# Causal attention on one core: key-by-query weights of a fifth row tile go through DRAM, and an early product moves into the next head

## The chip, the cores and the metric

One core of a Trainium2 chip runs the whole program as one launch. The metric is the device time in microseconds, median of the runs. The engines are TensorE (PE, with PEld for its weight loads), VectorE (DVE), ScalarE (ACT), GpSimd (POOL), and SyncE (SP), which here issues every DMA. Each engine works through its own instructions strictly in the order of its program, and waits for semaphores of the others.

## The reference

One transformer block with adaptive layer norm, in fp32:

```python
h = _layernorm(x) * (1 + ca) + sa
q, k = rope(h @ wq), rope(h @ wk); v = h @ wv     # 32 heads, 8 key/value heads, T = 1024, HD = 128
scores = einsum('bhtd,bhsd->bhts', q, k) / sqrt(HD), masked to s <= t
att = softmax(scores); out = einsum('bhts,bhsd->bhtd', att, v)
x = x + ga * (out @ wo)
h = _layernorm(x) * (1 + cb) + sb
x = x + gb * (h @ W.T + b + low-rank term of the rank that a router picks)
```

## The kernel before, in words

Every fp32 matrix product is made of three products in a rounded format (fp32r): hi x hi, hi x lo, lo x hi. So each operand is split by a copy on ScalarE (the `_hi` part) and a subtraction on VectorE (the `_lo` part).

The program runs over 8 groups (one key/value head each) of 4 query heads. A head h has a `front` and a `back` on every engine, one function each in the block of the engine; all of them name the same steps in orders that are written out by hand. The queries of a head are 8 row tiles i of 128, tile i with its i+1 key blocks:

- `scores(h, i)` on TensorE, `masked(h, i)` on VectorE (adds the mask, finds the row maximum), `exp(h, i)` on ScalarE, `inverse(h, i)` on VectorE, `normalise(h, i)` on GpSimd.
- The weights must then lie with the keys on the partitions. For tiles 0 to 3 VectorE transposes blocks of 32x32 (`turn`) into the buffer `turned`; SyncE writes it to DRAM (`p_rows`) and reads it back in column order into `pa_lo` (`turn_columns`: one write, a wait for its landing, four reads); ScalarE and VectorE split it (`early_hi`, `early_lo`). For tiles 4 to 7 TensorE transposes each block into the PSUM banks `transposed` (`transposes`), and ScalarE and VectorE split each bank into `pb_hi` and `pb_lo` (`transposed_hi`, `transposed_lo`).
- `weighted(h, 0)`, called pva, multiplies the values with `pa`: the early product, at the end of the head's `back`. `weighted(h, 1)`, called pvb, does it with `pb`: the late product, in the `front` of the next head, after its tile 3's scores. `output_hi`, `output_lo` split both results.
- Between them lie filling jobs (`fill`): projections of q, k, v for the next head or group, output projections (`wo`) in the first head of a group. Weights of the projections come through two slots of `stage`, in the order of the lists `W_GROUP` and `W_LATE`; `split_hi` and `split_lo` split them, and the split of the load two places before frees a slot.

SyncE's program is one queue too: its loads and the turning of the columns stand in one written order, and a wait for a landing holds up every issue behind it.

## Time and profile before

| | |
|---|---|
| median of 3 runs | 1114.86 us (1112.5 to 1119.03) |
| the profiled execution's own time | 1113.62 us |
| its span, first to last instruction | 1111.8 us, mean granted clock 0.993 |
| busy share of the span | PE 95%, DVE 70%, ACT 57%, POOL 47% |
| DMA | 88.22 MB in 99004 packets, 79 GB/s |

A row of time gives the start and the length of an operation in us, then engine, line, operation, output and inputs, shapes and count, and in brackets the engine's idle time before it with the instruction that ended it. Matrix products overlap a little in such rows, so what a step takes is read from start to start.

### The profile page before, as it was taken

To read this page: it belongs to the slowest core of one execution; us is meant where nothing else is said; L and a number is where in the kernel's file an instruction comes from. 1 tells how busy PE (TensorE), PEld (TensorE's weight loads), DVE (VectorE), ACT (ScalarE), POOL (GpSimd) and SP (SyncE) were. 2 spreads that over 40 slices of the span, in tenths; PEclk is the share of its full clock that TensorE was granted. 3 is DMA by queue.
4 is the path that set the end of the run, shared out by engine and by line. 5 is a ranking of instruction groups with operands and counts; after the bars stand their busy time and mean duration, and the time that the engine had idled before them with its cause. 6 is when DMAs were issued, how large, how long until landed. Compare 5 with 4: busy or idle time off the path is not lost.

```text
span 1111.8 us, 16527 instructions
## 1 busy us (share of the span) xinstructions
PE 1055.0 (95%) x5416; PEld 867.1 (78%) x5416; DVE 775.7 (70%) x1834; ACT 635.4 (57%) x1298; POOL 521.9 (47%) x506
## 2 busy tenths in 40 slices
PE   6999999998999989999999999999999999998897
PEld 3668878887878878887878878887878878887775
DVE  4668866588558866588557865678647865678576
ACT  5547754477337654477437754477436753477433
POOL 2535553365425654365425643365425652455244
PEclk8999999999999999999999999999999999999999
DMA  6562323133302233033202233033212223024001
GB/s 212 152 216 67 103 79 76 39 95 95 78 18 68 85 96 76 34 98 97 71 25 67 86 95 77 12 109 99 57 49 67 77 86 95 3 97 130 10 20 57
DMA packets 99004, 88.22 MB, mean 79 GB/s; under 512 B 39460, under 2 KB 84644, under 8 KB 98792
## 3 DMA queue, kind: packets, MB, share of 16 engines
q1 hardware_dynamic: 98920, 87.17, 26.6%
q8 instruction: 44, 0.72, 0.3%
q14 instruction: 40, 0.33, 0.1%
HBM read 59.88 MB, written 27.26 MB: 78 GB/s over the span
## 4 chain that ended last, share of the span: by engine, by line
PE 56%; DVE 14%; ACT 12%; POOL 7%; issue 6%; DMA 4%; SPq 1%; POOLq 0%; DVEq 0%; ACTq 0%
PE accumulators L649 14%; PE accumulators L664 13%; PE accumulators L679 13%; PE scores L609 6%; PE transposed L622 6%; DVE p_large L1172 3%; POOL qc L1539 3%; ACT pb_hi L907 2%; ACT pa_hi L913 2%; DVE turned L1196 2%; POOL qr L1535 2%; DVE pb_lo L1184 2%; ACT qr L932 2%; PE scores L864 2%; ACT qr L931 2%
## 5 line engine op out<-in xcount | busy, mean ns | idle before, releaser
L907 ACT ACTIVATE pb_hi<-transposed 128x512 fp32r<-128x512 f32 (+3 forms) x256 | 117.5, 511 | 211.7 <-PE transposed L622 211.5
L1526 POOL TENSOR_SCALAR p_large<-p_large,rowinv 128x640 f32<-128x640 f32 (+3 forms) x128 | 125.1, 978 | 229.0 <-DVE rowinv L1177 229.0
L1535 POOL TENSOR_TENSOR qr<-qr,trig 128x512 f32<-128x512 f32 x80 | 104.4, 1305 | 221.1 <-ACT qr L932 221.0
L1184 DVE TENSOR_TENSOR pb_lo<-transposed,pb_hi 128x512 fp32r<-128x512 f32 (+3 forms) x256 | 138.9, 584 | 94.0 <-ACT pb_hi L907 93.6
L899 ACT ACTIVATE p_large<-p_large,negmax 128x640 f32<-128x640 f32 (+3 forms) x128 | 126.3, 986 | 87.6 <-DVE negmax L1172 87.5
L609 PE MATMUL scores<-k_hi,q_hi 128*128 128x512 f32 (+2 forms) x384 | 139.3, 363 | 1.7 <-DVE negmax L1172 1.7
L1172 DVE CUSTOM_DVE_ANT_0 p_large<-scores,mask 128x640 f32<-128x640 f32 (+3 forms) x128 | 129.4, 1011 | 4.0 <-PE scores L609 3.7
L609 PE MATMUL scores<-k_hi,q_lo 128*128 128x512 f32 (+2 forms) x384 | 131.4, 342 | 0.0
L609 PE MATMUL scores<-k_lo,q_hi 128*128 128x512 f32 (+2 forms) x384 | 131.1, 341 | 0.0
L1526 POOL TENSOR_SCALAR p_small<-p_small,rowinv 128x128 f32<-128x128 f32 (+3 forms) x128 | 97.2, 775 | 71.6 <-DVE rowinv L1177 71.6
L622 PE MATMUL transposed<-ident,p_large 128*128 128x128 f32 x832 | 113.9, 275 | 12.3 <-DVE pb_lo L1184 6.1
L622 PEld LDWEIGHTS transposed<-ident,p_large 128*128 128x128 f32 x832 | 93.8, 140 | 38.2 <-POOL p_large L1526 16.2
L1539 POOL TENSOR_TENSOR qc<-qc,qr 128x512 f32<-128x512 f32 x80 | 119.9, 1499 | 6.5 <-POOL qr L1535 0.3
L1249 DVE TENSOR_TENSOR y<-accumulators,y 128x512 f32<-128x512 f32 x64 | 43.5, 688 | 84.4 <-PE accumulators L679 84.4
L1223 DVE TENSOR_TENSOR qc<-accumulators,trig 128x512 f32<-128x512 f32 x80 | 55.2, 690 | 45.5 <-ACT qr L932 45.4
L609 PEld LDWEIGHTS scores<-k_hi,q_hi 128*128 128x128 f32 x384 | 72.5, 189 | 7.9 <-DVE negmax L1172 2.2
L609 PEld LDWEIGHTS scores<-k_hi,q_lo 128*128 128x128 f32 x384 | 72.3, 188 | 6.7
L679 PE MATMUL accumulators<-wo_hi,o_hi 128*128 128x512 f32 x256 | 71.1, 399 | 6.3 <-DVE y L1249 3.9
L609 PEld LDWEIGHTS scores<-k_lo,q_hi 128*128 128x128 f32 x384 | 72.9, 190 | 5.0
L899 ACT ACTIVATE p_small<-p_small,negmax 128x128 f32<-128x128 f32 (+3 forms) x128 | 71.0, 562 | 7.8 <-DVE negmax L1172 6.8
L664 PE MATMUL accumulators<-h_hi,wq_hi 128*128 128x512 f32 x256 | 69.3, 392 | 1.3 <-DVE ga_b L1282 1.3
L679 PE MATMUL accumulators<-wo_lo,o_hi 128*128 128x512 f32 x256 | 68.6, 390 | 0.0
(165 smaller groups left out, 2225.9 us busy)
## 6 DMA issues: line engine op xcount, KB each, us to landing
p_rows<-turned SPq DMA_DIRECT2D x32, 640.0 KB, 2.9
pa_lo<-p_rows SPq DMA_DIRECT2D x128, 160.0 KB, 3.1
stage<-in_L_attn_wq_dram SPq DMA_DIRECT2D x32, 256.0 KB, 2.8
stage<-in_L_attn_wo_dram SPq DMA_DIRECT2D x32, 256.0 KB, 2.7
v_rows<-vt SPq DMA_DIRECT2D x32, 128.0 KB, 2.2
v_lo<-v_rows SPq DMA_DIRECT2D x32, 128.0 KB, 3.1
y<-in_L_wmod_dram SPq DMA_DIRECT2D x4, 512.0 KB, 5.7
stage<-in_L_attn_wk_dram SPq DMA_DIRECT2D x8, 256.0 KB, 2.7
```

Source lines behind the costliest of these rows:

```text
L609: mm = nc.tensor.matmul(S_flat[:, c0 + key:c0 + key + n], a[:, i * P:(i + 1) * P], b[:, key:key + n], start=(k == 0), stop=(k == 2))
L622: mm = nc.tensor.transpose(TB[:, b, (j % 4) * P:(j % 4 + 1) * P], row(i)[:, j * P:(j + 1) * P], ident[:])
L649: mm = nc.tensor.matmul(acc[:, c0:HALF], v[:, j, :], pt, start=(hi and v is v_hi and j == 0), stop=(not hi and j == 4 * half + 3))
L664: mm = nc.tensor.matmul(acc, a[:, k, :], b[:, k, half * HALF:(half + 1) * HALF], start=(n == 0), stop=(n == 3 * KC - 1))
L679: mm = nc.tensor.matmul(acc, a[:, r, t * P:(t + 1) * P], b[:, r, :], start=(n == 0), stop=(n == 3 * R - 1))
L899: nc.scalar.activation(row(i), row(i), ACT.Exp, bias=negmax[:, i:i + 1], scale=-1.0, accum_out=rowsum[:, i:i + 1]).then_inc(s_exp, 1)
L907: nc.scalar.activation(pt_of(i, part, True), src, ACT.Copy).then_inc(t_hi, 1)
L1172: nc.vector.tensor_tensor_reduce(row(i), S_flat[:, c0:c0 + n], mask[:, T - n:T], -SCALE, 3.4e38, ALU.add, ALU.min, negmax[:, i:i + 1]).the ...
L1184: nc.vector.tensor_tensor(pt_of(i, part, False), src, f32(pt_of(i, part, True)), ALU.subtract).then_inc(t_lo, 1)
L1526: nc.gpsimd.tensor_scalar(row(i), row(i), rowinv[:, i:i + 1], 1.0, ALU.mult, ALU.mult).then_inc(s_norm, 1)
L1535: nc.gpsimd.tensor_tensor(qr[:, s, :], qr[:, s, :], trig[:, 1, half * HALF:(half + 1) * HALF], ALU.mult).then_inc(r_sin, 1)
L1539: nc.gpsimd.tensor_tensor(qc[:, s, :], qc[:, s, :], qr[:, s, :], ALU.add).then_inc(r_sum, 1)
```

## The change

Tile 4's weights no longer pass through TensorE. After `normalise(h, 4)` VectorE transposes them in blocks into the first half of `turned` (`turn_fourth`; it waits until the write of `p_rows` for this head has landed, since that reads the same buffer), SyncE writes them to `fourth_rows` and reads them back into `pb_lo`, and `fourth_hi` and `fourth_lo` split them in the next head's front, ahead of `transposed_hi` and `transposed_lo` of tile 7. The late product waits for `fourth_lo`. `pb` is laid out by tile, in runs of 32 columns like `pa`. The early product moves from the end of `back` to the next head's front, before tile 7's transposes. Some steps change places: `masked(h, 4)` stands before `output_lo` for h > 0, `early_lo` stands behind the output projections' additions for h = 0, the k weights are loaded and split before the fourth `wo` block. The end of the last group is ordered anew in the same sense (not shown).

```diff
         def pt_of(i, part, hi):
 
             js = parts(i)[part]
-            n = len(js)
...
-            return buf[:, at:at + 3 * (n - 1) + 1:3, :]
+            at = 7 * (i - 4) + js[0]
+            return (pb_hi if hi else pb_lo)[:, :, at:at + len(js), :].rearrange("p a l r -> p l a r")
         def pt_row(j, half, hi):
 
...
                 at = 1 + ROW_START[j]
                 return j * P, buf[:, :, at:at + 4 - j, :].rearrange("p a i r -> p i a r")
             buf = pb_hi if hi else pb_lo
...
+            if j == 7:
+                return 2 * P, buf[:, :, 13:29:15, :].rearrange("p a i r -> p i a r")
+            i0 = max(4, j)
+            at = 7 * (i0 - 4) + j
+            return (i0 - 4) * P, buf[:, :, at:at + 7 * (7 - i0) + 1:7, :].rearrange("p a i r -> p i a r")
...
         W_FIRST = [("k", 0), ("q", 0), ("v", 0)]
         W_GROUP = [("q", 1), ("q", 2), ("wo", 0), ("q", 3), ("wo", 1), ("wo", 2)]
-        W_LATE = [("q", 0), ("wo", 3), ("k", 0), ("v", 0)]
+        W_LATE = [("q", 0), ("k", 0), ("wo", 3), ("v", 0)]
...
+            def turn_fourth(n):
+
+                sp.wait_ge(fourth_turned, n + 1)
+                if n:
+                    sp.wait_ge(fourth_in, 64 * n)
+                sp.dma_start(fourth_rows, turned[:, 0:5 * P]).then_inc(fourth_out, 16)
+                sp.wait_ge(fourth_out, 16 * (n + 1))
+                if n:
+                    sp.wait_ge(a_full, N.of[("a", ("pvb", (n - 1) % R), (n - 1) // R)])
+                src = fourth_rows.rearrange("(a c) (b m) -> b c a m", a=4, b=4)
+                for b in range(4):
+                    sp.dma_start(f32(fourth_blocks(pb_lo)[32 * b:32 * b + 32]), src[b]).then_inc(fourth_in, 16)
...
@@ -548,6 +561,7 @@
             turn_columns(0)
             sp.wait_ge(a_full, N.value("a", ("mod", "sb"), g0))
             sp.dma_start(mod_w[:, :, 0:D], wmod_v[:, :, 2 * D:3 * D]).then_inc(mod_in[1], 16)
+            turn_fourth(0)
             sp.wait_ge(a_full, N.value("a", ("mod", "cb"), g0))
             sp.dma_start(mod_w[:, :, D:2 * D], wmod_v[:, :, 5 * D:6 * D]).then_inc(mod_in[2], 16)
             load(("q", 2), g0)
@@ -563,21 +577,25 @@
                     turn_value_rows(at)
                     load(("wo", 0), at)
                     turn_columns(R * g)
+                    turn_fourth(R * g)
                 load(("q", 3), at)
                 turn_columns(R * g + 1)
+                turn_fourth(R * g + 1)
                 load(("wo", 1), at)
                 load(("wo", 2), at)
                 turn_columns(R * g + 2)
+                turn_fourth(R * g + 2)
                 if g + 1 < GROUPS:
                     load(("q", 0), at, 1)
+                    load(("k", 0), at, 1)
                     load(("wo", 3), at)
-                    load(("k", 0), at, 1)
...
                 turn_columns(R * g + 3)
+                turn_fourth(R * g + 3)
...
                     steps = [(pa_hi_done, n, hi_lo[:2], range(4)), (pa_lo_done, n, hi_lo[2:], range(4))]
                 else:
                     first, second = (N.value("t", (h, 7, part), at, ahead) for part in range(2))
+                    pe.wait_ge(fourth_lo_done, head_number(h, at, ahead) + 1)
                     steps = [(t_hi, first, hi_lo[:2], range(4)), (t_lo, first, hi_lo[2:], range(4)),
                              (t_lo, second, hi_lo, range(4, 8))]
...
@@ -720,6 +739,7 @@
                 fill(h, 1, at)
                 scores(h, 2, at)
                 if h or not at.first:
+                    weighted(hb, 0, at, ahead)
                     transposes(hb, 7, at, ahead)
                 scores(h, 3, at)
                 if h or not at.first:
...
                 scores(h, 5, at)
                 fill(h, 3, at)
                 fill(h, 4, at)
-                transposes(h, 4, at)
                 scores(h, 6, at)
                 transposes(h, 5, at)
                 scores(h, 7, at)
                 fill(h, 5, at)
                 transposes(h, 6, at)
-                weighted(h, 0, at)
```

On ScalarE and VectorE (an increment's end and a second copy of the same lines are left out):

```diff
             def front(h, at):
                 hb, ahead = before(h, at)
-                if h or not at.first:
-                    output_hi(hb, 0, at, ahead)
                 fill(h, 1, at)
-                if h or not at.first:
-                    transposed_hi(hb, 7, at, ahead)
                 exp(h, 0, at)
                 exp(h, 1, at)
+                if h or not at.first:
+                    fourth_hi(hb, at, ahead)
+                    transposed_hi(hb, 7, at, ahead)
+                    output_hi(hb, 0, at, ahead)
                 exp(h, 2, at)
...
+                    split_hi(("k", 0), at, 1)
                     split_hi(("wo", 3), at)
-                    split_hi(("k", 0), at, 1)
...
+                elif i == 6:
+                    row_free = (fourth_turned, head_number(h, at) + 1)
                 else:
-                    row_free = (t_full, N.value("t", (h, i - 2, 1), at))
+                    row_free = (t_full, N.value("t", (h, 5, 1), at))
...
@@ -1191,9 +1215,24 @@
                     if i in tiles:
                         need(dve, s_norm, N.value("s", (h, i), at))
                         if n and i == 0:
-                            dve.wait_ge(rows_out, 16 * n)
+                            dve.wait_ge(fourth_out, 16 * n)
                         src = row(i)[:, js[0] * P:(js[-1] + 1) * P].rearrange("p (j b c) -> p j b c", b=4, c=32)
                         nc.vector.transpose(turned_blocks(i, js), src).then_inc(p_turned, 1)
+
+            def turn_fourth(h, at):
+
+                n = head_number(h, at)
+                dve.wait_ge(s_norm, N.value("s", (h, 4), at))
+                dve.wait_ge(rows_out, 16 * (n + 1))
+                src = row(4).rearrange("p (j b c) -> p j b c", b=4, c=32)
+                dst = turned[:, 0:5 * P].rearrange("p (b l r) -> p l b r", b=4, r=32)
+                nc.vector.transpose(dst, src).then_inc(fourth_turned, 1)
+            def fourth_lo(h, at, ahead=0):
+                n = head_number(h, at, ahead)
+                dve.wait_ge(fourth_hi_done, n + 1)
+                nc.vector.tensor_tensor(fourth_blocks(pb_lo), f32(fourth_blocks(pb_lo)), f32(fourth_blocks(pb_hi)),
+                                        ALU.subtract).then_inc(fourth_lo_done, 1)
```

```diff
@@ -1307,15 +1346,16 @@
                     fill(hb, 5, at, slice(-1, None), -ahead)
                 masked(h, 0, at)
                 masked(h, 1, at)
-                if h or not at.first:
-                    output_lo(hb, 0, at, ahead)
                 fill(h, 1, at)
                 masked(h, 2, at)
+                inverse(h, 0, at)
+                inverse(h, 1, at)
                 if h or not at.first:
+                    fourth_lo(hb, at, ahead)
                     transposed_lo(hb, 7, at, ahead)
+                    output_lo(hb, 0, at, ahead)
                 masked(h, 3, at)
-                for i in range(3):
-                    inverse(h, i, at)
...
@@ -1326,9 +1366,12 @@
                 elif at.g + 1 < GROUPS:
                     split_lo(("q", 0), at, 1)
                 turn(h, at, 0, 1, 2)
+                if h:
+                    masked(h, 4, at)
                 if h or not at.first:
                     output_lo(hb, 1, at, ahead)
-                masked(h, 4, at)
+                if not h:
+                    masked(h, 4, at)
                 turn(h, at, 3)
...
                 fill(h, 4, at, slice(0, -1))
-                transposed_lo(h, 4, at)
+                turn_fourth(h, at)
                 masked(h, 6, at)
...
                 if last:
+                    split_lo(("k", 0), at, 1)
                     split_lo(("wo", 3), at)
-                    split_lo(("k", 0), at, 1)
...
-                early_lo(h, at)
+                if h:
+                    early_lo(h, at)
                 inverse(h, 7, at)
                 if h == 2:
                     split_lo(("wo", 2), at)
                 fill(h, 5, at, slice(0, -1))
+                if not h:
+                    early_lo(h, at)
```

Three places as the program's order has them. First VectorE's, in the front of head 3 of a group: from masked 1 (p_small 128x256) to masked 3 (128x512). Before:

```order
L1172 ISA p_small,negmax<-scores,mask 128x256
L1172 ISA negmax 128x1
L1215 TENSOR_TENSOR o_lo<-accumulators,o_hi 128x512
L1172 ISA p_small,negmax<-scores,mask 128x384
L1172 ISA negmax 128x1
L1184 TENSOR_TENSOR pb_lo<-transposed,pb_hi 128x4x128 x2
L1172 ISA p_small,negmax<-scores,mask 128x512
```

And after the change (its line numbers are shifted):

```order
L1196 ISA p_small,negmax<-scores,mask 128x256
L1196 ISA negmax 128x1
L1196 ISA p_small,negmax<-scores,mask 128x384
L1196 ISA negmax 128x1
L1201 RECIPROCAL rowinv<-rowsum 128x1 x2
L1234 TENSOR_TENSOR pb_lo<-pb_lo,pb_hi 128x4x160
L1208 TENSOR_TENSOR pb_lo<-transposed,pb_hi 128x4x4x32 x2
L1254 TENSOR_TENSOR o_lo<-accumulators,o_hi 128x512
L1196 ISA p_small,negmax<-scores,mask 128x512
```

The tile-7 subtractions (`pb_lo` from `transposed`) now stand behind two reciprocals (`inverse` 0 and 1) and the new subtraction, `fourth_lo`; `output_lo` of the early product (o_lo) stands behind them.

Second SyncE's queue, where one group ends and the next begins (`turn_columns` of head 3, the load of the next v weights, the q loads). Before:

```order
L514 DMA p_rows<-turned 128x1280
L520 DMA pa_lo<-p_rows 32x4x320 x4
L507 DMA stage<-in_L_attn_wv_dram 128x4x128
L507 DMA stage<-in_L_attn_wq_dram 128x4x128 x2
L529 DMA v_rows<-vt 32x4x256 x4
```

And after:

```order
L514 DMA p_rows<-turned 128x1280
L520 DMA pa_lo<-p_rows 32x4x320 x4
L527 DMA fourth_rows<-turned 128x640
L533 DMA pb_lo<-fourth_rows 32x4x160 x4
L507 DMA stage<-in_L_attn_wv_dram 128x4x128
L507 DMA stage<-in_L_attn_wq_dram 128x4x128 x2
L542 DMA v_rows<-vt 32x4x256 x4
```

The write and the four reads of `fourth_rows` now stand ahead of the load of the v weights.

Third TensorE's, in head 2's back, from the projection's last third to tile 5's transposes. Before:

```order
L664 MATMUL accumulators<-h_hi,wq_lo 128x512 x4
L622 MATMUL transposed<-ident,p_large 128x128 x5
L609 MATMUL scores<-k_hi,q_hi 128x512
L609 MATMUL scores<-k_lo,q_hi 128x512
L609 MATMUL scores<-k_hi,q_lo 128x512
L609 MATMUL scores<-k_hi,q_hi 128x384
L609 MATMUL scores<-k_lo,q_hi 128x384
L609 MATMUL scores<-k_hi,q_lo 128x384
L622 MATMUL transposed<-ident,p_large 128x128 x6
```

And after:

```order
L683 MATMUL accumulators<-h_hi,wq_lo 128x512 x4
L627 MATMUL scores<-k_hi,q_hi 128x512
L627 MATMUL scores<-k_lo,q_hi 128x512
L627 MATMUL scores<-k_hi,q_lo 128x512
L627 MATMUL scores<-k_hi,q_hi 128x384
L627 MATMUL scores<-k_lo,q_hi 128x384
L627 MATMUL scores<-k_hi,q_lo 128x384
L640 MATMUL transposed<-ident,p_large 128x128 x6
```

The five transposes of tile 4 ahead of tile 6's scores are gone.

## Rows read from the trace of the kernel before

**Rows 1.** The page, part 1: the line of TensorE's busy time.

```profile
PE 1055.0 (95%) x5416; PEld 867.1 (78%) x5416; DVE 775.7 (70%) x1834; ACT 635.4 (57%) x1298; POOL 521.9 (47%) x506
```

**Rows 2.** TensorE's longest wait inside the groups: us in total, times, longest us.

```profile
PE accumulators L664 <- DVE wk_lo L1261: 14.2, 7, 2.0
```

**Rows 3.** TensorE in order of time (start, us): the late products of one group.

```profile
461.58 1.07 PE L649 MATMUL accumulators<-pb_hi,v_hi 128*128 128x512 f32 x4
...
483.92 1.09 PE L649 MATMUL accumulators<-pb_hi,v_hi 128*128 128x512 f32 x4
...
506.28 1.09 PE L649 MATMUL accumulators<-pb_hi,v_hi 128*128 128x512 f32 x4
...
542.53 1.16 PE L649 MATMUL accumulators<-pb_hi,v_hi 128*128 128x512 f32 x4
...
587.33 1.07 PE L649 MATMUL accumulators<-pb_hi,v_hi 128*128 128x512 f32 x4
```

**Rows 4.** TensorE in order of time, round tile 4's transposes of head 2.

```profile
493.55 0.76 PE L622 MATMUL transposed<-ident,p_large 128*128 128x128 f32 x5
494.07 0.47 PE L609 MATMUL scores<-k_hi,q_hi 128*128 128x512 f32 x1
...
495.71 0.85 PE L622 MATMUL transposed<-ident,p_large 128*128 128x128 f32 x6 [0.17 <-DVE pb_lo L1184]
```

**Rows 5.** TensorE in order of time, the last output projection of head 0.

```profile
573.16 1.20 PE L679 MATMUL accumulators<-wo_hi,o_hi 128*128 128x512 f32 x4 [0.54 <-DVE y L1249]
```

**Rows 6.** VectorE in order of time: masked 0, masked 6, masked 0.

```profile
482.64 0.28 DVE L1172 CUSTOM_DVE_ANT_0 p_small<-scores,mask 128x128 f32<-128x128 f32 x1
...
495.76 1.09 DVE L1172 CUSTOM_DVE_ANT_0 p_large<-scores,mask 128x896 f32<-128x896 f32 x1
...
505.51 0.28 DVE L1172 CUSTOM_DVE_ANT_0 p_small<-scores,mask 128x128 f32<-128x128 f32 x1
```

**Rows 7.** Busy us of each engine from masked 6 to masked 0.

```profile
495.76:505.51 9.75, 9.75 (x61) 8.60 (x61) 9.15 (x17) 9.10 (x17) 6.13 (x6) 1.00 0.43 112
```

**Rows 8.** SyncE's DMA issues in order of time.

```profile
491.59 0.33 SPq L514 DMA_DIRECT2D p_rows<-turned  x1
494.53 1.75 SPq L520 DMA_DIRECT2D pa_lo<-p_rows  x4
...
520.88 0.40 SPq L507 DMA_DIRECT2D stage<-in_L_attn_wv_dram  x1
```

**Rows 9.** ScalarE in time: exp 0, exp 2, then the v weights' split.

```profile
506.35 0.41 ACT L899 ACTIVATE p_small<-p_small,negmax 128x128 f32<-128x128 f32 x1
...
507.26 0.62 ACT L899 ACTIVATE p_small<-p_small,negmax 128x384 f32<-128x384 f32 x1
...
523.65 0.63 ACT L961 ACTIVATE wv_hi<-stage 128x512 fp32r<-128x512 f32 x1 [1.02 <-DMA stage<-in_L_attn_wv_dram]
```

**Rows 10.** Groups by form (busy us, mean ns): the nearest to the new operations.

```profile
L1201 DVE TENSOR_TENSOR pa_lo<-pa_lo,pa_hi 128x1280 fp32r<-128x1280 f32 x32 | 47.7, 1490 | 5.9 <-ACT pa_hi L913 5.8
L913 ACT ACTIVATE pa_hi<-pa_lo 128x1280 fp32r<-128x1280 f32 x32 | 40.4, 1262 | 0.7 <-DMA pa_lo<-p_rows 0.7
L1196 DVE STREAM_TRANSPOSE turned<-p_small 128x256 f32<-128x256 f32 x128 | 48.9, 417 | 0.3
```

**Rows 11.** DMA issues by form: KB each, median us from issue to landing.

```profile
v_rows<-vt SPq DMA_DIRECT2D x32, 128.0 KB, 2.2
...
y<-in_L_wmod_dram SPq DMA_DIRECT2D x2, 1024.0 KB, 8.1
```

**Rows 12.** First group: a gate weight load on SyncE, then TensorE's next projection.

```profile
59.87 0.51 SPq L552 DMA_DIRECT2D y<-in_L_wmod_dram  x1
...
75.35 1.19 PE L664 MATMUL accumulators<-h_hi,wq_hi 128*128 128x512 f32 x4 [1.27 <-DVE ga_b L1282]
```

**Rows 13.** Busy us by stretch near the start, with the granted clock (PEclk).

```profile
19.93:22.64 2.71, 0.10 (x2) 0.03 (x1) 0.69 (x1) 2.71 (x6) 0.00 (x0) 0.63 0.00 0
22.64:27.40 4.76, 4.68 (x18) 3.40 (x19) 3.13 (x5) 4.76 (x10) 0.00 (x0) 0.50 0.00 0
```

98 lines of the change are left out of this document (48 added, 50 removed).

## The prediction

> **What bounds the kernel now.** I read the page's part 1 first: TensorE is busy 95% of the span [rows 1], so time can leave only with TensorE's own work or with its waits, and a new wait adds to the time directly. Next the list of waits: the largest inside the groups is that for the low part of the k weights, 14.2 us in 7 waits, once between two groups [rows 2]. Third, TensorE in order of time, marked off at the late products. Those of one group start at 461.58, 483.92, 506.28, 542.53 and 587.33 [rows 3]. They stand in the fronts of heads 1, 2, 3, 0 and 1, so the four stretches are A = 22.34 (head 1 to 2), B = 22.36 (2 to 3), C = 36.25 (3 to the next group's 0) and D = 44.80 (0 to 1). A and B occur 8 times each, C and D 7 times. Fourth, VectorE by stretch: in B, from masked 6 to the next front's masked 0 it is busy 9.15 of 9.75 us, and ScalarE 9.10 [rows 7]. TensorE sets the pace there, but the two side engines stand close behind. Last, SyncE's queue: rows out at 491.59, read back from 494.53 (the write took 2.94), 1.75 for four reads [rows 8].
>
> **The change, A and B.** TensorE loses tile 4's five transposes: 494.07 - 493.55 = 0.52 us per head, and a wait of 0.17 behind them [rows 4]. The early product costs the same at its new place. The new layout of `pb` is that of `pa`, which the early product reads already, so I price it at nothing. TensorE alone would thus take 0.7 to 1.4 less per head. But the late product now waits for `fourth_lo`, at the end of a chain on the side engines:
>
> - VectorE turns tile 4 only when the write of `p_rows` has landed: 494.53 - 483.92 = 10.61 after the late product [rows 3, 8]. The transpose of 640 columns by the one of 256 (417 ns [rows 10], the fixed part counted once) takes 0.85; bounds 0.7 and 1.04. So masked 6, queued behind it, starts at 11.5 instead of 495.76 - 483.92 = 11.84 [rows 3, 6]: 0.3 earlier, though scores 6 come 0.5 earlier.
> - From masked 6 to masked 0 VectorE has 0.6 idle at most to give back [rows 7]. The pair that splits tile 4 leaves this stretch and later returns as `fourth_lo`; masked 4 and `early_lo` change places without changing the sum. So masked 0 comes 0.3 to 0.9 earlier.
> - After masked 0: its 0.28 [rows 6]; exp 0 and exp 1 take 507.26 - 506.35 = 0.91 [rows 9]; then `fourth_hi`, half of `pa_hi`'s 1262 ns and a little, 0.7; `fourth_lo`, half of `pa_lo`'s 1490 ns and a little, 0.82 [rows 10]; 0.14 for the hand-overs. The late product starts 2.85 after masked 0. Before it started 506.28 - 505.51 = 0.77 after it in B and 483.92 - 482.64 = 1.28 in A [rows 3, 6].
>
> B grows by 2.85 - 0.77 = 2.08 less 0.3 to 0.9, so 1.2 to 1.8; I take 1.5. A grows by 1.57 less the same, 0.7 to 1.3; I take 1.0. Eight times 2.5 is **+20 us**; the ends give +15 and +25. TensorE's saving is lost in that wait.
>
> **C.** Loading k before the fourth `wo` block shrinks the wait of 2.0. But SyncE's queue now has the fourth turn ahead of the v load. In before the v load is issued 520.88 - 506.28 = 14.6 after head 3's late product, and its split starts at 523.65 - 506.28 = 17.37 [rows 3, 8, 9]. Now: rows landed 10.6, four reads 1.75, the write of 320 KB 2.2 to 2.94 (the 128 KB write took 2.2 [rows 11], the 640 KB one 2.94 [rows 8]), four reads 1.75, so the v load goes out at 16.4 to 17.1 and, 2.77 later, its split starts at 19.2 to 19.9. ScalarE stands in order behind that split with head 3's last exps, and the v projection waits for it; what k's earlier load saves and what the transposes save is waited out there, some 4 to 5 us in one piece. C grows by 1.9 to 2.7; I take 2.3. The Trainium skill (DMA: Bandwidth & Descriptors, Anatomy of one DMA) gives, for GpSimd's path, some 2.0 us fixed and bytes over 436e3 per us: by an estimate from it the 320 KB write takes 2.75, inside my two bounds, though the 640 KB one would take 3.5 where the trace has 2.94.
>
> **D.** The group's first head has the most work for TensorE and no such wait ahead of its late product: it loses the 0.52, the 0.17, and the wait of 0.54 for y, since `early_lo` now stands behind those additions [rows 4, 5]. That is 1.2 to 1.6 less; I take 1.3. C and D together: 7 x (2.3 - 1.3) = **+7 us**; the ends give +2 and +10.
>
> **The first group.** `turn_fourth(0)` stands in SyncE's queue ahead of the gate weights' last load, issued at 59.87 and landing in 8.1 [rows 11, 12]. It needs at least a write and reads, 2.2 + 1.75, and waits for tile 4 of head 0 too; I estimate the load 6.8 later, so landed at 74.8, with its product and the projection of 75.35 behind: **+3 us**, between 0 and 5. The tail's new order: 0, between -3 and +3, as its pieces are the same.
>
> **Sum** against the profiled execution's own 1113.6, which is 1.2 under the median: 1113.6 + 20 + 7 + 3 = 1143.6, say 1143. With all bounds at their ends: 1128 to 1157.
>
> **Rivals.**
>
> *The clock falls* (0.20). The 4 to 5 us idle before the v projection is longer than any idle inside the groups now, 2.0 at most [rows 2]. Near the start TensorE was busy 0.10 of 2.71 us, at a granted clock of 0.63, and then ran 4.76 us at 0.50, the lower level of 1.2 GHz [rows 13]. As that stretch was all but full, it cost half of it, 2.4 us. Seven times gives +17: 1160. The skill (TensorE: Matmul & The Clock Gate, Part 1: The HAM clock gate) states that the clock falls back when the engine has been idle for a while, by which such waits would be paid twice. The waits of 2.0 left the clock alone, which is why I don't put it higher.
>
> *TensorE keeps the pace; the kernel gets faster* (0.13). If masked 0 comes 2.1 earlier in B and 1.6 in A, the late product is not late; it decides there. For it: TensorE's work is shorter, so all scores come earlier, and some of the 9.15 busy may be overlapped starts. Against: only 0.6 idle is there to close up. With A and B at 21.0 (-1.35, sixteen times: -22), C -1.8 and D -1.7 (7 x -3.5 = -25): 1067; part of it gives up to 1109.
>
> *The v load is hidden* (0.12). If the slot or another work ends later than SyncE's new queue, C falls by 1.0, not grows: 7 x (-3.3) = -23, so 1120. Against: before, ScalarE already waited 1.02 for this very load [rows 9].
>
> *The side chain costs a fourth of what I say* (0.10): 1113.6 + 5 + 7 + 3 = 1129, or 1117 where D saves more and the first group nothing. That the change doesn't do what it says can be left out: the program's order shows the transposes gone.
>
> **The numbers.** My forecast has 0.45. Faster by over 0.5% (under 1109.3) is the second rival, with a little of the tail's: 0.14. Within 0.5%, to 1120.4, about what a measurement of this kernel can tell from no change: half of the third rival and a part of the fourth, 0.10. Slower: 0.76. The range takes in the forecast's bounds, the clock's 1160 with its own ends, and reaches down to the hidden load: 1117 to 1163; outside are the faster case and a little of both ends.
>
> **What would show it.** After: a wait of TensorE for `fourth_lo` (`pb_lo` from `pb_lo`, 4x160 elements) ahead of the late product, about 2 us in heads 2 and 3; VectorE idle on the write of `p_rows` ahead of the turn of tile 4; intervals A 23.3, B 23.9, C 38.5, D 43.5; the k wait gone and 4 to 5 us ahead of the v projection; ScalarE idle 3 to 4 us on the v load; clock 1.00 in that stretch. I am wrong if A and B are below 22.3 (the chain is shorter than priced, or VectorE had more to give), if C shrinks, or if a stretch behind the v wait has a clock of 0.5.

## The result, and the profile after

The changed kernel takes 1211.58 us (median of 4 runs, 1207.2 to 1212.03), the kernel before 1116.51 beside it: ratio 1.084, 95% interval 1.0805 to 1.0875. The direction was as forecast; the size, +95 us instead of +28, lies outside the range.

The page of the kernel after, its head and the line of busy times:

```profile
span 1205.4 us, 16397 instructions
...
PE 1065.8 (88%) x5256; PEld 869.4 (72%) x5256; DVE 811.8 (67%) x1834; ACT 632.9 (53%) x1266; POOL 519.6 (43%) x506
```

TensorE did 160 instructions fewer and was busy longer, 1065.8 us against 1055.0 [rows 1]: a part of its work ran at a lower clock. The rest of the loss is waits. The profiled execution is the fastest of the four (its span 1205.4 us against 1111.8 before), and all rows below are of single executions. The list of TensorE's waits after (us in total, times, longest), to be read beside [rows 2]:

```profile
PE accumulators L683 <- DVE qc L1262: 42.0, 7, 6.5
PE accumulators L668 <- ACT pb_hi L924: 29.4, 17, 2.0
PE transposed L640 <- POOL p_large L1573: 23.4, 41, 3.0
PE accumulators L683 <- DVE wk_lo L1300: 8.7, 7, 1.9
```

The first is the wait ahead of the v projection, 4.7 to 6.5 us in each of 7 groups; the second stands ahead of the late product; the third, 4.5 us in before, stands for the most part ahead of tile 5's and 6's transposes.

The list names ScalarE's `pb_hi` for the second wait, but the late product waits for two things, the first half of tile 7's `pb_hi` and `fourth_lo`, and `fourth_lo` is the later one. VectorE in order of time has it end at 686.36, and TensorE starts at 686.46; the first half of `pb_hi` was done at 685.98:

```profile
685.53 0.83 DVE L1234 TENSOR_TENSOR pb_lo<-pb_lo,pb_hi 128x640 fp32r<-128x640 f32 x1 [0.46 <-ACT pb_hi L930]
```

Now TensorE in order of time, the late products of one group, in the same order as [rows 3]:

```profile
593.65 1.17 PE L668 MATMUL accumulators<-pb_hi,v_hi 128*128 128x512 f32 x4 [0.73 <-issue]
...
637.45 1.10 PE L668 MATMUL accumulators<-pb_hi,v_hi 128*128 128x512 f32 x4
...
661.67 1.17 PE L668 MATMUL accumulators<-pb_hi,v_hi 128*128 128x512 f32 x4 [1.64 <-ACT pb_hi L924]
...
686.46 2.02 PE L668 MATMUL accumulators<-pb_hi,v_hi 128*128 128x512 f32 x4 [2.00 <-ACT pb_hi L924]
```

Read from start to start, D is 43.80, A 24.22, B 24.79; the next group's first late product is at 732.37, so C is 45.91. Over the whole span, summed from these starts: A +15.8 us (8 times), B +19.2 (8), C +56.2 (7), D -7.0 (7), the stretch ahead of the first late product +5.4, the last head's way to the tail +4.1, the tail itself 0. Together 93.7; the spans differ by 93.6. C alone is 60% of it.

What happens in C is seen on SyncE. Its issues in order of time, after head 3's late product:

```profile
696.23 0.34 SPq L514 DMA_DIRECT2D p_rows<-turned  x1
699.19 1.75 SPq L520 DMA_DIRECT2D pa_lo<-p_rows  x4
701.03 0.38 SPq L527 DMA_DIRECT2D fourth_rows<-turned  x1
705.20 1.73 SPq L533 DMA_DIRECT2D pb_lo<-fourth_rows  x4
706.97 0.43 SPq L507 DMA_DIRECT2D stage<-in_L_attn_wv_dram  x1
```

The write of `fourth_rows` went out at 701.03 and had landed at 705.20: 4.17 us for 320 KB, right behind four reads, where the 640 KB of `p_rows` took 2.96. What stands ahead of it is what lengthens it: the same write of a group's head 0 has no reads just before it (the last ones went out 4.8 to 5.3 us earlier) and took 2.17 to 2.19 in all seven groups, as in SyncE's rows of the group before:

```profile
613.15 0.34 SPq L527 DMA_DIRECT2D fourth_rows<-turned  x1
615.34 1.73 SPq L533 DMA_DIRECT2D pb_lo<-fourth_rows  x4
```

The v load left 20.5 us after the late product, in before 14.6 [rows 3, 8]. ScalarE waited for it, and TensorE for what stands behind it on ScalarE and VectorE:

```profile
710.09 0.63 ACT L984 ACTIVATE wv_hi<-stage 128x512 fp32r<-128x512 f32 x1 [5.33 <-DMA stage<-in_L_attn_wv_dram]
```

```profile
703.09 1.16 PE L683 MATMUL accumulators<-h_hi,wk_hi 128*128 128x512 f32 x4 [1.35 <-DVE wk_lo L1300]
...
715.01 2.07 PE L683 MATMUL accumulators<-h_hi,wv_hi 128*128 128x512 f32 x4 [6.21 <-DVE qc L1262]
```

Four products of 128x512 took 1.16 us there and 2.07 us here. The windows of that stretch (busy us of PE, PEld, DVE, ACT, POOL, then TensorE's granted clock):

```profile
684.46:686.46 2.00, 0.00 (x1) 0.03 (x1) 1.38 (x6) 2.00 (x6) 2.00 (x2) 1.00 0.00 0
686.46:690.00 3.54, 3.54 (x9) 2.79 (x10) 3.13 (x8) 2.81 (x8) 1.43 (x3) 0.52 0.03 7
...
708.80:715.01 6.21, 0.00 (x1) 0.01 (x1) 2.95 (x4) 4.85 (x8) 1.33 (x2) 0.90 0.38 113
715.01:720.29 5.28, 5.28 (x12) 4.12 (x13) 0.69 (x1) 1.06 (x2) 4.80 (x4) 0.50 0.00 0
```

In this group the clock fell twice: after the 2.00 us idle ahead of head 3's late product, and after the 6.21 us idle ahead of the v projection, each time to the lower level, 1.2 GHz. (In two of the seven groups it fell only at the v projection; see experiment nine.) That the clock falls back when the engine stands idle is what the Trainium skill (TensorE: Matmul & The Clock Gate, Part 1: The HAM clock gate) states; the trace agrees for the 6 us waits, while of seven idle stretches of 2.0 us two left the clock at 1.00.

### The profile page after: what moved, and what is told of

The parts are those of the page before. It is cut to its first block, busy times and chain, and to the rows that moved or that the text cites. A ratio compares the mean times of both kernels' runs of the same rounds, so it can differ in the third digit from the quotient of the medians.

```text
span 1205.4 us, 16397 instructions
## 1 busy us (share of the span) xinstructions
PE 1065.8 (88%) x5256; PEld 869.4 (72%) x5256; DVE 811.8 (67%) x1834; ACT 632.9 (53%) x1266; POOL 519.6 (43%) x506
## 4 chain that ended last, share of the span: by engine, by line
PE 49%; ACT 14%; DMA 11%; DVE 11%; issue 8%; POOL 4%; SPq 2%; DVEq 0%; POOLq 0%; ACTq 0%
PE accumulators L668 14%; PE accumulators L698 12%; PE accumulators L683 10%; PE scores L627 6%; DMA p_rows<-turned 6%; POOL qc L1586 4%; ACT pa_hi L936 3%; ACT p_large L916 3%; DMA fourth_rows<-turned 2%; ACT pb_hi L924 2%; PE transposed L640 2%; DVE p_large L1196 2%; DVE turned L1220 2%; DMA stage<-in_L_attn_wv_dram 2%; PE scores L881 2%
## 5 line engine op out<-in xcount | busy, mean ns | idle before, releaser
L924 ACT ACTIVATE pb_hi<-transposed 128x512 fp32r<-128x512 f32 x192 | 92.4, 532 | 117.1 <-PE transposed L640 116.6
L1208 DVE TENSOR_TENSOR pb_lo<-transposed,pb_hi 128x512 fp32r<-128x512 f32 x192 | 110.4, 616 | 40.4 <-ACT pb_hi L924 40.0
L1573 POOL TENSOR_SCALAR p_small<-p_small,rowinv 128x128 f32<-128x128 f32 (+3 forms) x128 | 92.9, 731 | 83.8 <-DVE rowinv L1201 79.5
L1586 POOL TENSOR_TENSOR qc<-qc,qr 128x512 f32<-128x512 f32 x80 | 117.1, 1463 | 26.5 <-DVE qc L1262 22.6
L640 PE MATMUL transposed<-ident,p_large 128*128 128x128 f32 x672 | 92.0, 277 | 24.0 <-POOL p_large L1573 23.4
L640 PEld LDWEIGHTS transposed<-ident,p_large 128*128 128x128 f32 x672 | 74.9, 141 | 42.1 <-POOL p_large L1573 39.5
L668 PE MATMUL accumulators<-pb_hi,v_hi 128*128 128x512 f32 (+2 forms) x256 | 65.7, 380 | 34.6 <-ACT pb_hi L924 29.4
L954 ACT ACTIVATE qr<-accumulators 64x512 f32<-64x512 f32 x80 | 47.6, 595 | 90.6 <-PE accumulators L683 89.0
L668 PEld LDWEIGHTS accumulators<-pb_hi,v_hi 128*128 128x128 f32 x256 | 48.0, 197 | 52.6 <-issue 44.3
L1262 DVE TENSOR_TENSOR qc<-accumulators,trig 128x512 f32<-128x512 f32 x80 | 55.1, 689 | 35.1 <-ACT qr L955 34.9
```

The lines of the kernel that those rows point to most:

```text
L640: mm = nc.tensor.transpose(TB[:, b, (j % 4) * P:(j % 4 + 1) * P], row(i)[:, j * P:(j + 1) * P], ident[:])
L668: mm = nc.tensor.matmul(acc[:, c0:HALF], v[:, j, :], pt, start=(hi and v is v_hi and j == 0), stop=(not hi and j == 4 * half + 3))
L924: nc.scalar.activation(pt_of(i, part, True), src, ACT.Copy).then_inc(t_hi, 1)
L1208: nc.vector.tensor_tensor(pt_of(i, part, False), src, f32(pt_of(i, part, True)), ALU.subtract).then_inc(t_lo, 1)
L1573: nc.gpsimd.tensor_scalar(row(i), row(i), rowinv[:, i:i + 1], 1.0, ALU.mult, ALU.mult).then_inc(s_norm, 1)
L1586: nc.gpsimd.tensor_tensor(qc[:, s, :], qc[:, s, :], qr[:, s, :], ALU.add).then_inc(r_sum, 1)
```

## The experiments

All medians are of 4 to 6 runs; "before" ran beside each, at 1117 to 1119 us. The table gives the time, the ratio to before with its 95% interval, and the median length of each stretch, worked out from the starts of the late products in each trace. A trace is of one execution, which need not be the median one: own place was profiled at 1214.1 us, both with own place at 1153.8. The two kernels with a short `fourth_lo` leave out a part of the computation.

| run | us | ratio | A | B | C | D |
|---|---|---|---|---|---|---|
| before | 1116.5 | 1 | 22.34 | 22.37 | 36.25 | 44.82 |
| after | 1211.6 | 1.084 (1.0805-1.0875) | 24.21 | 24.80 | 44.75 | 43.80 |
| v load first | 1176.7 | 1.0527 (1.0503-1.055) | 24.24 | 24.82 | 40.37 | 43.79 |
| pair early | 1197.8 | 1.0722 (1.0704-1.0741) | 23.94 | 23.99 | 43.28 | 45.06 |
| both | 1164.9 | 1.0437 (1.0409-1.0465) | 23.96 | 23.98 | 37.41 | 45.06 |
| moved product alone | 1121.8 | 1.0047 (1.0031-1.0063) | 22.52 | 22.76 | 36.31 | 44.89 |
| all but tile 4's way | 1123.3 | 1.0045 (1.003-1.0061) | 22.53 | 22.78 | 36.32 | 44.64 |
| idle filled, behind the wait | 1242.5 | 1.1107 (1.1079-1.1134) | 24.19 | 24.89 | 48.31 | 45.21 |
| idle filled, ahead of it | 1199.3 | 1.0727 (1.0687-1.0767) | 24.19 | 24.78 | 41.84 | 45.17 |
| own place | 1208.4 | 1.0809 (1.0776-1.0842) | 24.05 | 26.25 | 43.99 | 43.79 |
| own place, pair early, merged writes | 1184.0 | 1.0579 (1.0557-1.0601) | 24.38 | 24.19 | 40.04 | 45.03 |
| both, tile 5 late | 1162.3 | 1.040 (1.036-1.0439) | 24.18 | 23.97 | 38.45 | 45.01 |
| the same, output_lo first | 1166.3 | 1.043 (1.0377-1.0483) | 24.56 | 24.38 | 38.54 | 45.02 |
| both, short fourth_lo | 1162.7 | 1.0383 (1.0337-1.0429) | 23.48 | 23.88 | 39.61 | 45.13 |
| both, short fourth_lo and turn | 1158.7 | 1.037 (1.0333-1.0408) | 23.48 | 23.74 | 37.55 | 45.10 |
| all but tile 4's way, a subtraction more | 1134.3 | 1.0163 (1.0125-1.0201) | 22.53 | 23.24 | 37.06 | 44.64 |
| the same, a copy more too | 1139.0 | 1.0187 (1.0159-1.0215) | 22.56 | 23.35 | 38.57 | 44.61 |
| both, own place | 1160.5 | 1.0368 (1.0337-1.0399) | 23.79 | 23.73 | 36.82 | 44.99 |

**One: the v load ahead of tile 4's turn.**

```diff
                 turn_columns(R * g + 3)
-                turn_fourth(R * g + 3)
+                if g + 1 == GROUPS:
+                    turn_fourth(R * g + 3)
...
                     load(("v", 0), at)
+                    turn_fourth(R * g - 1)
```

> The changed kernel, with one difference: on SyncE the next group's v load goes out ahead of head 3's turn of tile 4. Theory Q (the queue): the v load then waits for its slot alone and goes out some 4 us earlier, so the wait of TensorE ahead of the v projection falls from 6 to about 2 us, the clock stays at 1.00 behind it (another 2.5 us), and C falls by 6.5: 7 times that is 45, so about 1166 us. Rival S (the side chain): the v projection waits for VectorE's rotation, which is late for other reasons; the v load's place gives less than 1 us a group, and the time stays above 1200.

35 us came back by the medians instead of 45; in the traces C is 31 less, 4.4 a group instead of 6.5. The wait ahead of the v projection went from 6.0 to about 2.1 (4.1 in the first group). The queue's theory holds for the wait. Its second half, that the clock stays at 1.00 behind it, does not: in six of the seven groups the v projection still began at 0.50 to 0.70. Two of the seven, with waits of 2.14 and 2.13 us:

```profile
697.56:700.06 2.50, 2.50 (x6) 2.02 (x7) 0.69 (x1) 0.49 (x2) 2.42 (x3) 0.50 0.34 98
831.16:833.66 2.50, 2.50 (x11) 2.05 (x12) 0.69 (x1) 0.45 (x2) 2.42 (x3) 1.00 0.32 95
```

**Two: the pair early.**

```diff
                 fill(h, 1, at)
+                if h or not at.first:
+                    fourth_hi(hb, at, ahead)
+                    transposed_hi(hb, 7, at, ahead)
                 exp(h, 0, at)
                 exp(h, 1, at)
...
                 masked(h, 1, at)
+                if h or not at.first:
+                    fourth_lo(hb, at, ahead)
                 fill(h, 1, at)
```

> The changed kernel, with one difference: fourth_hi and tile 7's transposed_hi stand ahead of exp 0 on ScalarE, and fourth_lo right behind masked 1 on VectorE. Theory C (the chain masked 0, exp 0, exp 1, fourth_hi, fourth_lo holds the late product): the wait ahead of it goes from 1.6 to 2.0 us to about 0.3, A and B fall by 1.5 each (24 us), and where head 3's late product ran at the lower clock another 1.7 a group comes back: about 1175 us. Rival: exp 0 moves 0.8 us later, with it all that follows on the side engines, and the gain is given back: above 1200.

14 us, less than half of what was expected. The wait ahead of the late product shrank as expected, to 0.6 at most, but A fell by 0.3 and B by 0.8 only, and D rose by 1.3 (with both edits the list of waits has one for `k_lo` ahead of scores, 8.1 us in 7). What the chain had cost was, for the most part, owed elsewhere too: TensorE's waits for GpSimd's normalised tiles ahead of its transposes rose from 23.4 us in after to 38.4.

**Three: both.**

> Both edits together. If the queue and the chain are separate costs, their gains add: 1211 less 45 less 36, about 1130 us. If both only remove the same loss (one wait takes the other's place), it is near the better of the two.

46.7 us, against 34.9 and 13.7 for the two alone: the gains add, though to 1165 and not to the 1130 that larger gains would have given. C is 37.41, nearly that of before. Two groups of the profiled execution waited 4.4 and 3.8 us ahead of the v projection and had C = 40.7 and 41.3; those that waited 2.0 to 2.5 had 36.8 to 39.0. The clock behind the two long waits was 0.50; of the five others one had 0.73 and four 1.00.

**Four: the moved product alone.** The move of `weighted(h, 0)` and its `output_` steps, made in the kernel before.

> The kernel before, with one part of the change alone: the early product moves from the end of a head's back to the next head's front, with output_hi and output_lo of it behind tile 7's transposed halves. If the move by itself costs nothing, 1112 to 1120 us. If it takes away a filling job in front of the scores of the next head, so that the late product or tile 7's transposes wait, 0.5 to 1 us a head more: 1130 to 1145.

+0.5%, A +0.2 and B +0.4: small, and less than the "if" of its expectation. Summed over the 16 stretches it is 4.6 us.

**Five: TensorE's idle time filled.** Besides the 20 products below, 6 stand ahead of the wait of each late product but the group's last.

```diff
                 bank_free(name, at, ahead)
+                if name == ("v", 0) and at.g + ahead > 0:
+                    for k in range(20):
+                        nc.tensor.matmul(ACC[:, N.slot("a", name, at, ahead), :], h_hi[:, 0, 0:P],
+                                         h_hi[:, k % KC, 0:HALF], start=True, stop=True)
                 pe.wait_ge(w_lo, w_number((kind, head), at, ahead))
```

> The changed kernel, and besides TensorE gets products that nobody reads: 20 (128x512, h_hi by h_hi) ahead of its wait for the v weights, into the bank that the v projection starts anew, and 6 ahead of the wait of each late product but the group's last. Theory K (the clock): TensorE's lower clock behind the v wait costs 2.5 us and that of head 3's late product 1.7 us a group, and both come from the idle time ahead of them; filled, the clock is 1.00 in both places, C falls by some 4, and the time by 7 x 4.2 = 29, to about 1182 us. Rival: the lower clock has another cause (the products at hand, the load of the chip), so the clock stays at 0.5 there and the time stays at 1211 or rises.

A miss in its making: 31 us slower. The wait ahead of the v projection isn't that for the weights but `bank_free`, for the accumulator that VectorE's `qc` rotation frees, and the 20 products stood behind it (TensorE in order of time, this run):

```profile
739.86 7.50 PE L682 MATMUL accumulators<-h_hi 128*128 128x512 f32 x20 [5.77 <-DVE qc L1269]
747.20 1.08 PE L690 MATMUL accumulators<-h_hi,wv_hi 128*128 128x512 f32 x4
```

They ran at the lower clock in the v projection's stead. It taught what TensorE waits for there.

**Six: all parts but tile 4's way.**

> The changed kernel's other parts without its first: tile 4's weights still go through TensorE's transposes as before; the early product has moved, k's weights come before the fourth wo block, masked 4 and early_lo change places. If the loss is all in tile 4's way through DRAM, this is near the run with the moved product alone, 1110 to 1125 us. If the order of k and wo costs something at the v load (its slot comes free later), C grows by 1 or more and it is above 1130.

1123.3, as the moved product alone. All but some 5 us of the 95 come from tile 4's way through DRAM. The order of k and wo costs nothing: the k wait of 2.0 became one of 1.6 to 2.1 ahead of the v projection (3.4 in one group, with a clock of 0.62 behind it).

**Seven: own place.**

```diff
-                sp.dma_start(fourth_rows, turned[:, 0:5 * P]).then_inc(fourth_out, 16)
+                sp.dma_start(fourth_rows, p_small[:, 5 * P:10 * P]).then_inc(fourth_out, 16)
...
-                dve.wait_ge(rows_out, 16 * (n + 1))
```

> The changed kernel, with one difference: tile 4 is turned into the half of p_small that tiles 2 and 3 have left, not into turned. So VectorE's turn of tile 4 needs no landing of p_rows, and turn 0 of the next head waits for p_rows' landing alone; masked 2 and 3 of the next head wait for the landing of fourth_rows instead, which is long past. Theory C: VectorE's wait of 0.9 us for the landing, with masked 6 behind it, is on the ring that sets A and B: they fall by 0.9 each, and the time by 15, to about 1196 us. Rival: masked 0 is held by the rotation of q instead, and A and B move by less than 0.3: 1206 or more.

Three us, within the measurement's width: the rival holds. Masked 6 did come earlier, but GpSimd works without a break from tile 5's normalise to tile 6's (a weight block's scaling, the rotation of q), so tile 6's transposes did not. B even grew, for here head 2's late product, after waits of 1.96 to 1.99 us, fell to the low clock in six of eight groups, with 4.0 to 4.4 us for its first twelve products instead of 2.9.

**Eight: own place, early pair, merged writes.** SyncE issues both writes before it waits for either.

> Own place for tile 4, the fourth pair ahead of exp 0 and masked 2, and on SyncE the write of fourth_rows behind the write of p_rows, ahead of the wait for its landing. If queue, chain and landing are all of the loss: the v load goes out at about 15 after head 3's late product as in before, C is at 36 to 37, A and B at 22.5 to 23, and the time 1110 to 1130 us. If a ring on the side engines remains, A and B stay above 23.5 and it is at 1140 or more.

The ring remained (A and B above 24), and C is 40: the v load left 15.7 us after the late product, but behind eight reads, and took 3.75 us to ScalarE; the waits ahead of the v projection were 3.6 to 4.5 us and the clock fell in all seven. Putting the v load first was worth more.

**Nine: the idle time filled where it is.** As five, but 26 products into a free bank of `transposed`, ahead of `bank_free`.

> The changed kernel with products that nobody reads, now where TensorE really stands idle: 26 (128x512) into a free bank of transposed ahead of the wait for the v projection's accumulator, and 6 ahead of each late product but the group's last. Theory K (the clock is a cost of its own): the v projection runs at clock 1.00, 2.8 us instead of 5.3, head 3's late product 1.7 us faster, so C falls from 45.4 to about 41; D pays 1.3 for its six, which fill no wait there. 7 x (-4.2 + 1.3) = -20: about 1191 us. Rival: what waits behind the v projection is late anyway (the k rotation, tile 6), and C falls by less than 1.5: above 1205.

12 us, of the 20 expected. The windows of this run round the same late product and v projection:

```profile
688.20:691.70 3.50, 3.49 (x16) 2.94 (x17) 3.18 (x8) 2.77 (x8) 1.50 (x3) 1.00 0.01 2
...
715.34:720.00 4.66, 4.66 (x20) 3.86 (x21) 1.98 (x3) 1.07 (x2) 4.50 (x4) 1.00 0.00 0
```

Clock 1.00 in both, and in this group C is 41.84 where it was 45.91: 4.1 less, near the 4.2 that was expected. Over all groups C fell by 16.9 us, 2.4 a group, since the late product had lost less elsewhere: the windows of the kernel after give 0.50 at the start of all seven v projections, but behind head 3's late products 0.71, 0.54, 1.00, 1.00, 0.51, 0.67 and 0.50. The filling itself took back 9.5 us in D (the six products there fill no wait) and 3.9 ahead of the first late product. So the clock is a cost of its own, some 17 of C's 56 us, and idle time is its cause; in the one group where 1.81 us of idle time were left ahead of the v projection, the clock behind it was 0.81. The 17 are from two executions that differ by 4 us, where the medians differ by 12, so they may be low.

**Ten and eleven: tile 5 late; then output_lo first.** `transposes(h, 5)` behind `scores(h, 7)`; in eleven also `output_lo(hb, 1)` ahead of `masked(h, 4)`.

> The run with both edits (v load first, fourth pair early), and tile 5's transposes behind tile 7's scores instead of ahead of them. Theory N (the saving of tile 4's transposes came back as a wait of tile 5's for GpSimd's normalise, 1.2 us): that wait goes, A and B fall by 1.0 to 1.2 each, the time by 16 to 19 from 1165, to about 1147. Rival R (a ring through VectorE, late product, scores 4, masks, turns, masked 0, fourth pair, sets A and B): TensorE reaches the next wait 1.2 sooner and waits there, A and B stay within 0.3.

> As the run before it, and output_lo of the late product ahead of masked 4 as in the kernel before. Ring R: VectorE's turn 3 and so the write of p_rows, the turn of tile 4 and masked 6 come by up to 0.6 earlier or later with this order; if the 0.6 of output_lo ahead of masked 5 is on the ring, A and B fall by up to 0.6 (10 us); if masked 4 is the one that is waited for, they rise by as much.

In ten the wait of 1.2 to 1.6 ahead of tile 5's transposes fell to 0.2, and that ahead of tile 6's grew from 0.3 to 1.65: A and B stayed within 0.3, as the ring's theory said. Eleven is 4 us slower than ten with overlapping intervals: inconclusive for the time, though A rose by 0.4.

**Twelve and thirteen: VectorE relieved.** Both kernels leave out work: four fifths of `fourth_lo`, in thirteen also of the turn of tile 4.

> The run with both edits, but fourth_lo subtracts only 128 of its 640 columns (a fifth; the rest of tile 4's low part stays unsplit, so this kernel leaves out part of the computation). VectorE's part falls from 0.85 to about 0.3. Ring R: A and B fall by 0.5 each, the time by 8 and what C has of it, to about 1153. If the late product was held by TensorE's waits for GpSimd alone: within 3 us of 1165.

> The run without most of fourth_lo, and turn_fourth turns 128 of tile 4's 640 columns too (both leave out four fifths of tile 4's turning and splitting). VectorE has 1.1 us a head less than in the run with both edits. Theory V (VectorE's added work is on the ring that sets A and B): A and B fall by 0.6 to 1.1 from 23.9, below 23.3. Theory W (the waits do it: masked 6 stands behind the landing of p_rows whatever the turn takes): A and B stay at 23.5 to 23.9.

A fell by 0.5 and B by 0.1, then 0.2; twelve's time is not told apart from that of "both", thirteen's is 6 us less. Twelve's round did not get shorter. VectorE's masked 3 still came 4.01 us after masked 0 in head 2, and masked 0 again 23.99 after masked 0, both as in experiment three. A fell only because head 2's late product now starts 1.09 after masked 0 instead of 1.51, and C rose by 2.2. VectorE in order of time, twelve, shows what took the place of the time saved:

```profile
648.00 0.17 DVE L1204 RECIPROCAL rowinv<-rowsum 128x1 f32<-128x1 f32 x1 [0.31 <-ACT p_small L918]
648.48 0.16 DVE L1204 RECIPROCAL rowinv<-rowsum 128x1 f32<-128x1 f32 x1 [0.32 <-ACT p_small L918]
648.56 1.27 DVE L1211 TENSOR_TENSOR pb_lo<-transposed,pb_hi 128x512 fp32r<-128x512 f32 x2
```

The two reciprocals (`inverse` 0 and 1), which the change put ahead of tile 7's subtractions, wait for exp 0 and exp 1 on ScalarE, and there `fourth_hi` and tile 7's copies stand ahead of both. So theory V does not hold for `fourth_lo` at this place. Thirteen's round in head 2, masked 0 to masked 0, is 23.73, 0.25 shorter: less than theory V's 0.6 at the least.

**Fourteen and sixteen: the pair put into the kernel without tile 4's way.**

```diff
                 masked(h, 1, at)
+                if h or not at.first:
+                    dve.wait_ge(rows_out, 16 * (head_number(hb, at, ahead) + 1))
+                    nc.vector.tensor_tensor(turned[:, 0:5 * P], turned[:, 0:5 * P], turned[:, 5 * P:10 * P],
+                                            ALU.subtract).then_inc(extra_done, 1)
```

> The kernel with all parts of the change but tile 4's new way (A 22.5, B 22.8), and one subtraction of 640 columns more on VectorE behind masked 1 in each front, which nobody reads. It measures what 0.85 us of VectorE costs at this place. Theory V: nearly all of it shows, A and B rise by 0.6 to 0.9 each, the time by 10 to 16, to about 1136. Theory W: what follows has room, A and B rise by less than 0.3, and the time is under 1130.

> As the run with one subtraction more, and also one copy of 640 columns on ScalarE ahead of tile 7's transposed_hi, for which the subtraction waits: the pair of the change at its early place, with nobody waiting for its data. If the time that the pair takes on the two side engines is what holds A and B, they rise from 22.5 and 22.8 to 23.5 or more, and the time to 1145 or above. If it is the rest of the way (TensorE's cover of tile 5 gone, the turn of tile 4), A and B stay below 23.2 and the time is under 1140.

A stayed and B rose by 0.5, then 0.6; C rose by 0.7 and 2.3. Fourteen lies between its two theories. Sixteen, at 1139, falls on its second side by the time and by A, with B 0.15 over that bound: the pair's time on the side engines is the smaller part of what holds A and B. It costs 11 to 16 us of the whole, more of it in C (8 to 13 us, summed from the starts) than in B (3 to 4).

**Fifteen: both, own place.**

> The run with both edits (v load first, fourth pair early), and tile 4 turned into p_small's free half, so that VectorE waits for no landing of p_rows. Theory W: the 0.9 us of that wait comes off A and B, to 23.0, and the time falls by 14, to about 1150. If GpSimd's row of operations between the normalise of tiles 5 and 6 holds the ring (masked 6 has room behind it), A and B stay within 0.3 of 23.9 and the time within 4 of 1165.

1160.5, the fastest kernel with the whole of tile 4's way; its interval overlaps that of "both", and its rival held: A and B stayed within 0.3. C is 36.82, the landing's wait is worth 0.2 in A and B. None beats the kernel before.

## Why the prediction was wrong

**The foreseen waits came; their sizes, and two costs that stood outside the sum, did not.** TensorE's saving was lost in a wait for `fourth_lo`; VectorE did wait for the landing of `p_rows`; the v load did go out late, with ScalarE idle 5.3 us; D shrank, by 1.0 (forecast 1.3); the new operations took 843 ns (turn, forecast 850), 722 (`fourth_hi`, 700) and 1022 (`fourth_lo`, 820). These are the groups by form of the kernel after:

```profile
L1234 DVE TENSOR_TENSOR pb_lo<-pb_lo,pb_hi 128x640 fp32r<-128x640 f32 x32 | 32.7, 1022 | 10.2 <-ACT pb_hi L930 10.2
L1229 DVE STREAM_TRANSPOSE turned<-p_large 128x640 f32<-128x640 f32 x32 | 27.0, 843 | 24.4 <-DMA p_rows<-turned 21.7 <-POOL p_large L1573 2.6
L930 ACT ACTIVATE pb_hi<-pb_lo 128x640 fp32r<-128x640 f32 x32 | 23.1, 722 | 0.0
```

**C was mis-sized most: 8.0 a group (56.2 in 7) instead of 2.3.** The v projection began 28.0 after head 3's late product, in before 22.7 (means of 7), which is 5.3; its first twelve products took 4.6 instead of 2.8 at the low clock; and head 0's late product, for which no wait was foreseen, waited 0.73 for a `fourth_lo` of 1.75. Two steps of the queue's sum failed. First "the write of 320 KB 2.2 to 2.94": the bounds came from writes that stood alone, and the one that stands alone did take 2.17, but this one is issued right behind four reads and took 3.9 in the median of those 24, 4.17 in the group shown. Second "rows landed 10.6": taken from head 2, while in head 3 it was 12.7 (699.19 - 686.46), since that head's own late product ran at the low clock and VectorE waited behind it (11.1 in a group where the clock stayed at 1.00, where the v load left at 18.9). Together the v load left at 20.5 where 16.4 to 17.1 was forecast. By experiment one, its place in the queue is worth 31 of C's 56 us.

**The clock rival came true besides, not instead.** It was held at 0.20 and as an alternative, and the forecast's own text put the clock there at 1.00; it is a consequence of the forecast's 4 to 5 us wait, and cost 17 us by experiment nine. That this is the amount worked out for it is in part luck: the 17 were for the v projection alone, 2.4 a group, where the twelve products lost 1.8 a group, 12 us in all; the rest is the second place, which the rival missed, the wait ahead of the late product that the forecast itself put at 2 us. At the v projection the clock fell in every group. That waits of 2.03 us in before left the clock alone was the argument against it; in after those of 2.00 did so in two groups of seven only.

**A and B: 35.0 us instead of 20.** "The late product starts 2.85 after masked 0" held (masked 0 at 683.56, so 2.90). Two steps failed. "The early product costs the same at its new place" was a term put at nothing: the move cost 4.6 us in A and B (experiment four). And "masked 0 comes 0.3 to 0.9 earlier" failed: it came 21.89 after the late product in B, in before 21.59, so 0.3 later. VectorE in order of time, masked 0, masked 5 and masked 0 of the kernel after:

```profile
658.77 0.28 DVE L1196 CUSTOM_DVE_ANT_0 p_small<-scores,mask 128x128 f32<-128x128 f32 x1
...
669.76 0.92 DVE L1196 CUSTOM_DVE_ANT_0 p_large<-scores,mask 128x768 f32<-128x768 f32 x1
...
683.56 0.28 DVE L1196 CUSTOM_DVE_ANT_0 p_small<-scores,mask 128x128 f32<-128x128 f32 x1
```

Before, masked 5 of the same head as in [rows 6]:

```profile
491.48 0.92 DVE L1172 CUSTOM_DVE_ANT_0 p_large<-scores,mask 128x768 f32<-128x768 f32 x1
```

From masked 5 to masked 0 it is 13.80 us and was 14.03: a little was given back there, as the prediction said. But from masked 0 to masked 5 it is 10.99 and was 8.84. The prediction counted `fourth_lo` as leaving the one stretch and did not count it, with the waits round it, as it came back in the other. The rows' landing came later too, 11.14 after the late product and not 10.61, since `output_lo` now stands between masked 4 and turn 3, and so masked 6 came at 12.24 (673.91) and not at 11.5; SyncE's rows:

```profile
669.87 0.33 SPq L514 DMA_DIRECT2D p_rows<-turned  x1
672.81 1.75 SPq L520 DMA_DIRECT2D pa_lo<-p_rows  x4
```

**What remains open.** With the early pair (experiment three) A and B are still 1.6 longer than before, though the late product waits 0.6 at most. Masked 0, the split of the q weights, masked 5 and masked 0 there:

```profile
642.97 0.28 DVE L1199 CUSTOM_DVE_ANT_0 p_small<-scores,mask 128x128 f32<-128x128 f32 x1
...
649.07 1.08 DVE L1303 TENSOR_TENSOR wq_lo<-stage,wq_hi 128x512 fp32r<-128x512 f32 x1 [0.36 <-ACT wq_hi L986]
...
653.15 0.91 DVE L1199 CUSTOM_DVE_ANT_0 p_large<-scores,mask 128x768 f32<-128x768 f32 x1
...
666.94 0.28 DVE L1199 CUSTOM_DVE_ANT_0 p_small<-scores,mask 128x128 f32<-128x128 f32 x1
```

From masked 0 to masked 5 it was 8.84 us and is 10.18; from masked 5 to masked 0 it was 14.03 and is 13.79. The growth is in the front. Of its 1.34, 0.39 is the q weights' split, which took 0.69 before, and the rest stands ahead of masked 3, where two things now hold VectorE: `fourth_lo`, and the reciprocals that wait for ScalarE. Take away most of `fourth_lo`, and the reciprocals wait in its stead (experiment twelve); put its time alone into the kernel without tile 4's way, and B grows by 0.5 (fourteen). The reciprocals' place was not tried by itself, and neither was GpSimd's row between tiles 5 and 6; how the 1.6 divides among them, the moved product (0.2 and 0.4) and the turn's landing (0.2) was not settled.

**The small terms.** The first group cost 5.4 instead of 3; the way from the last group's head 3 to the tail's late product 4.1 instead of 0.

## What to carry to other kernels

Where an engine is 95% busy, taking 0.5 us of its work a head is worth little more than that, and here giving its work to DMA and to two engines that are 94% busy in the same stretch cost more. Follow an operation that is moved to the stretch where it arrives, and not only out of the one that it leaves, and ask of each wait that moves with it what stands behind it. In a queue that waits for landings, place the load with a reader first (here 35 us), and price a write by one in the same place in the queue: 2.2 us alone was 3.9 behind four reads. And a wait on TensorE can have two prices, its length and the clock behind it: if a forecast contains such waits, the clock's cost belongs to the forecast, not to a rival.

## What the runs showed of the hardware

- The 320 KB write took 2.17 to 2.19 us in the seven places where nothing was issued just before it, 3.5 to 4.4 (median 3.9) in the 24 right behind four reads, and 3.2 to 5.6 right behind the v load (experiment three; 3.44 in the group shown), while the 640 KB write took 2.9 alone. With the writes ahead of the reads (experiment eight) it landed in 2.4. SyncE's issues in experiment three:

```profile
683.86 0.40 SPq L507 DMA_DIRECT2D stage<-in_L_attn_wv_dram  x1
684.36 0.45 SPq L527 DMA_DIRECT2D fourth_rows<-turned  x1
687.80 1.74 SPq L533 DMA_DIRECT2D pb_lo<-fourth_rows  x4
```

- A wait of 2.00 us was followed by a granted clock of 0.52 in one place, and one of 2.03 in before by 1.00 in another. At one and the same place, the v projection of experiment one, waits of 2.14 and 2.13 us were followed by 0.50 and 1.00. The length of the wait alone does not decide it. Nor do the groups of one run agree: C of the kernel after lay between 43.1 and 45.9.
- `fourth_lo` took 0.83 us in heads 2 and 3 (685.53) and 1.75 at the start of a group (730.52): a mean of 1022 ns for one form hides two. At 730.52 it began while GpSimd's rotation of q was running, and it ended 0.69 after that one's end at 731.58. Where VectorE's operation was the first to begin, as `wk_lo` at 702.26, it took its usual 0.68 and GpSimd's, begun 0.23 later, took 1.60 instead of 1.29. GpSimd and VectorE in order of time:

```profile
730.29 1.29 POOL L1586 TENSOR_TENSOR qc<-qc,qr 128x512 f32<-128x512 f32 x1
730.52 1.75 DVE L1234 TENSOR_TENSOR pb_lo<-pb_lo,pb_hi 128x640 fp32r<-128x640 f32 x1 [0.34 <-ACT pb_hi L930]
```
